# GpSimd makes the gated products of two FFN units in one instruction, with a ring of six units

## The chip, the core and the metric

The kernel runs on one core of one Trainium2 chip. The metric is the device time of one execution in microseconds (us). The profile's names of the engines are used beside the full ones: PE is TensorE (matmuls and transposes; PEld its weight loads), DVE is VectorE, ACT is ScalarE, POOL is GpSimd, SP is SyncE, which issues the DMAs here. Each engine takes its instructions in the order in which the kernel lists them for it; between engines only semaphores hold. So a late instruction delays everything behind it on its engine.

## The reference, cut to what matters

The input x has 8 images of 192 channels and 256 tokens. One layer norm and a delta-rule attention (12 heads of 16, chunks of 16 tokens) are followed by a second layer norm and a mixture-of-experts FFN:

```python
x = x + _L0_conv_ref(_ln_c(x), Wq, Wk, Wv, Wb, Wo)      # S_t = S_{t-1} + k_t u_t^T, o_t = S_t^T q_t, per head
t = _to_tokens(x)
t = t + _L0_ffn_ref(_ln_t(t), router_w, w_gate, w_up, w_down, ws_gate, ws_up, ws_down, sg_w, sg_b)
...
probs = jax.nn.softmax(x @ router_w, axis=-1)
gates, idx = jax.lax.top_k(probs, TOPK_ROUTED)           # 2 of E = 8 experts
g = jax.nn.silu(jnp.einsum('bsd,edh->bseh', x, w_gate))  # H = 192
u = jnp.einsum('bsd,edh->bseh', x, w_up)
expert_out = jnp.einsum('bseh,ehd->bsed', g * u, w_down)
routed = jnp.einsum('bse,bsed->bsd', dense_g, expert_out)
shared = jax.nn.silu(x @ ws_gate) * (x @ ws_up) @ ws_down  # HS = 768
alpha = jax.nn.sigmoid(x @ sg_w + sg_b)
return alpha * shared + (1.0 - alpha) * routed
```

All in float32. The kernel computes all eight experts for every token and gives the unselected ones a weight of zero. The `g * u` of the experts and of the shared part are the gated products that the change is about.

## The kernel before

The 256 tokens are cut into 16 chunks of 16 tokens; with 8 images a chunk has 128 rows, one for each partition. A software pipeline runs over steps c (about -3 to 18, a function `step(c, par)` for each engine): in step c the projections and norms of chunk c+3 and c+2 are made (functions `A_...`), the recurrence of chunk c runs, the attention output and second norm of chunk c-1 (`Fa_...`), and the FFN of chunks c-1 and c-2 (`Fb_...`, `unit`, `hidden`, `Fc_...`). `at(d, fn, ...)` calls fn for chunk c+d. In each `step` the order of the work of its engine is written out by hand.

**VectorE** runs the recurrence: 16 tokens of a chunk, four instructions each (L1425, L1427, L1429, L1433), which make 64 slots; the small jobs of the other stages stand between them at fixed slots (`others`). Slot 0 needs `fill` 0 of its chunk, a TensorE matmul (L403) that brings the keys into PSUM; slot 23 needs the attention output that GpSimd has summed (`Fa_otok`, L1238); slot 32 has the statistics of the second norm, slot 36 its bias (L1162), slot 43 the split of the normed tokens, slots 47 to 58 the router.

**The FFN** of a chunk has 12 units of 192 hidden columns (8 experts, 4 quarters of the shared part). For each unit TensorE makes gate and up (`Fb_up`, five matmuls, the last of them L440), ScalarE copies both to SBUF (`unit`: L713 silu, L714 scale) and GpSimd multiplies them (`hidden` on GpSimd, L1008). The copies go to a ring of `RING = 4` places in `sg` and `ug`: `unit` m waits until the product of unit m-4 has been made. The products go to `hid`, which holds half a chunk, six units. TensorE turns `hid` in five groups of up to four 128-column blocks (`Fb_turn` g, L448), all into one PSUM bank; ScalarE copies the bank (`hidden` g on ScalarE, L724); TensorE multiplies by the down weights (`Fb_down` g, L463). Turn g waits for the copy of turn g-1, and for as many units as its blocks cover: 3, 6, 8, 11 and 12 of them.

**GpSimd** also multiplies the states with the queries and sums them, in two halves for a chunk: `reading` (L963, two instructions) and `summing` (L970 three times, then L987). It makes `rs` for both norms (`rsqrt`, L952) and scales k, q and v (`A_kn`, `A_qn`, `A_vn` L920, `A_klo`). Its order in a steady step is: product 6, `rsqrt`, product 7, `reading` 0, products 8, 9, 10, `summing` 0, `A_kn`, product 11, `A_qn`, product 0 of the next chunk, `reading` 1, `summing` 1, `A_vn`, products 1 to 5, `A_klo`.

**ScalarE** has in the middle of a step two table loads (L748) around the exponentials and logarithms; in the order before, unit 11 stands behind them:

```python
at(-2, unit, 10)
at(-2, hidden, 1)
at(-3, Fc_out)
table(c + 2, LN_EXP)
at(2, A_inv)
table(c - 1, LN_EXP)
at(-1, Fa_exp)
table(0, SILU)
at(-2, hidden, 2)
at(-2, unit, 11)
at(-1, unit, 0)
```

**TensorE**'s order around it is: `Fb_turn` 1, `Fb_up` 11, `fill` 6, `Fb_up` 0 of the next chunk, `Fb_turn` 2, `Fb_down` 0, `fill` 7, `Fb_down` 1, `Fb_turn` 3, `Fb_down` 2, `fill` 0 of the next chunk, and so on.

Of the kernel before, what the change touches and what calls it, by code (L numbers as in the profile page):

```python
# [6 lines left out]
ALU = mybir.AluOpType  # L7
# [11 lines left out]
E, H, HS = 8, 192, 768  # L19
UN = E + HS // H  # L20
# [1 line left out]
KT = HID // P  # L22
GRP = [(0, 4), (4, 8), (8, 12), (12, 16), (16, 18)]
NG = len(GRP)
RING = 4
R = E + 2
NQK, NVB = 2 * C, C + NH
EARLY = 14
# [6 lines left out]
def build(nc, x, Wq, Wk, Wv, Wb, Wo, router_w, w_gate, w_up, w_down, ws_gate, ws_up, ws_down, sg_w, sg_b, out):  # L35
    ctx = ExitStack()
    with ctx:
# [51 lines left out]
        h = sb("h", [P, 2 * P])  # L89
# [474 lines left out]
        def _(act):  # L564
# [179 lines left out]
            def step(c, par):  # L744
                def table(n, name):

                    if (0 <= n < NC) and tables[0] != name:
                        nc.scalar.preload_act_table_set(name)  # L748
                        tables[0] = name

                at = partial(stage, c, par)
                if c == -3:
                    at(3, A_xs)
                    at(3, A_plus)
                    at(3, A_h)
                    at(3, A_xh)
                    at(3, A_hT)
                elif c == -2:
                    at(3, A_xs)
                    at(2, A_silu_v)  # L760
                    at(2, A_silu_qk)
                    at(2, A_sq)
                    table(0, LN_EXP)
                    at(2, A_inv)
                    at(2, A_khi)
                    at(3, A_plus)
                    at(3, A_h)
                    at(3, A_xh)
                    at(2, place, 0)
                    at(2, place, 1)  # L770
                    at(3, A_hT)
                    weights_hi0(5)
                    weights_hi0(6)
                elif c == -1:
                    at(3, A_xs)
                    weights_hi0(7)
                    weights_hi0(8)
                    table(0, SILU)
                    at(2, A_silu_v)
                    at(2, A_silu_qk)  # L780
                    weights_hi0(9)
                    at(2, A_sq)
                    table(0, LN_EXP)
                    at(2, A_inv)
                    at(3, A_plus)
                    weights_hi0(10)
                    at(3, A_h)
                    at(3, A_xh)
                    at(2, A_khi)
                    weights_hi0(11)  # L790
                    weights_hi1(0)
                    at(3, A_hT)
                    weights_hi1(1)
                    weights_hi1(2)
                elif c == 0:
                    weights_hi1(3)
                    at(3, A_xs)
                    table(0, SILU)
                    at(2, A_silu_v)
                    at(2, A_silu_qk)  # L800
                    at(2, A_sq)
                    weights_hi1(4)
                    weights_hi1(5)
                    at(1, place, 0)
                    table(0, LN_EXP)
                    at(2, A_inv)
                    at(3, A_plus)
                    weights_hi1(6)
                    weights_hi1(7)
                    at(3, A_h)  # L810
                    at(3, A_xh)
                    weights_hi1(8)
                    at(2, A_khi)
                    at(3, A_hT)
                elif c < NC:
                    if c == 1:
                        table(0, SILU)
                    if c > 1:
                        at(1, A_khi)
                    at(3, A_xs)  # L820
                    at(0, place, 1)
                    once(c, 1, weights_hi1, 9)
                    at(-2, unit, 3)
                    at(-2, unit, 4)
                    at(2, A_silu_qk)
                    at(2, A_sq)
                    at(2, A_silu_v)
                    once(c, 1, weights_hi1, 10)
                    at(-1, Fa_oc)
                    at(-2, unit, 5)  # L830
                    at(-2, unit, 6)
                    at(-2, hidden, 0)
                    at(-3, Fc_res)
                    at(-2, unit, 7)
                    once(c, 1, weights_hi1, 11)
                    at(-2, unit, 8)
                    at(-1, Fa_x1)
                    at(-1, Fa_h)
                    at(-2, unit, 9)
                    at(1, place, 0)  # L840
                    at(3, A_plus)
                    at(-1, Fa_hT)
                    at(-2, unit, 10)
                    at(-2, hidden, 1)
                    at(-3, Fc_out)
                    table(c + 2, LN_EXP)
                    at(2, A_inv)
                    table(c - 1, LN_EXP)
                    at(-1, Fa_exp)
                    table(0, SILU)  # L850
                    at(-2, hidden, 2)
                    at(-2, unit, 11)
                    at(-1, unit, 0)
                    at(3, A_h)
                    at(3, A_xh)
                    at(-2, hidden, 3)
                    at(-1, unit, 1)
                    at(-1, unit, 2)
                    at(3, A_hT)
                    at(-2, hidden, 4)  # L860
                else:
                    at(-2, unit, 3)
                    at(-2, unit, 4)
                    at(-3, Fc_res)
                    at(-1, Fa_oc)
                    at(-2, unit, 5)
                    at(-2, unit, 6)
                    at(-2, hidden, 0)
                    at(-2, unit, 7)
                    at(-2, unit, 8)  # L870
                    at(-1, Fa_x1)
                    at(-3, Fc_out)
                    at(-1, Fa_h)
                    at(-2, hidden, 1)
                    at(-2, unit, 9)
                    at(-1, Fa_hT)
# [7 lines that stand above are left out]
                    at(-1, unit, 1)  # L884
                    at(-2, hidden, 3)
                    at(-1, unit, 2)
                    at(-2, hidden, 4)
# [10 lines left out]
        def _(pool):  # L898
# [99 lines left out]
                tt(W1[:, columns(m)], raw1[:, columns(m)], spare(m), ALU.subtract).then_inc(s_w1, 1)  # L998

            def hidden(q, p, m):  # L1000
                pool.wait_ge(s_ug, q * UN + (m + 1))

                if m >= UN // 2 or later(q, 1):
                    last = ((m - UN // 2) % UN + 1) * H - 1
                    g = [lo * P <= last < hi * P for lo, hi in GRP].index(True)
                    pool.wait_ge(s_ht, q * NG + (g + 1 - (0 if m >= UN // 2 else NG)))
                r = m % (UN // 2)
                tt(hid[:, r * H:(r + 1) * H], sg[:, m % RING], ug[:, m % RING], ALU.mult).then_inc(s_hid, 1)  # L1008

            def step(c, par):  # L1010
                at = partial(stage, c, par)
# [39 lines left out]
                    weights_1(8)  # L1051
                elif c < NC:
                    once(c, 1, weights_1, 9)
                    at(-2, hidden, 6)
                    if c <= NC:
                        rsqrt(c)
                    at(-2, hidden, 7)
                    once(c, 1, weights_1, 10)
                    once(c, 1, weights_1, 11)
                    at(0, reading, 0)  # L1060
                    at(-2, hidden, 8)
                    at(-2, hidden, 9)
                    at(-2, hidden, 10)
                    at(0, summing, 0)
                    at(2, A_kn)
                    at(-2, hidden, 11)
                    at(2, A_qn)
                    at(-1, hidden, 0)
                    at(0, reading, 1)
                    at(0, summing, 1)  # L1070
                    at(2, A_vn)
                    at(-1, hidden, 1)
                    at(-1, hidden, 2)
                    at(-1, hidden, 3)
                    at(-1, hidden, 4)
                    at(-1, hidden, 5)
                    at(2, A_klo)
                else:
                    at(-2, hidden, 6)
                    if c <= NC:  # L1080
                        rsqrt(c)
                    at(-2, hidden, 7)
                    at(-2, hidden, 8)
                    at(-2, hidden, 9)
                    at(-2, hidden, 10)
                    at(-2, hidden, 11)
                    at(-1, hidden, 0)
                    at(-1, hidden, 1)
                    at(-1, hidden, 2)
                    at(-1, hidden, 3)  # L1090
                    at(-1, hidden, 4)
                    at(-1, hidden, 5)

            pool.memset(ident[:, :], 0.0).then_inc(s_id, 1)
            pool.wait_ge(s_id, 1)
# [378 lines left out]
```

## Time and profile before

| | |
|---|---|
| median of 3 runs | 482.03 us (480.83 to 482.6) |
| profiled execution | 479.88 us, of which the span from first to last instruction is 478.1 us |
| busy share of the span | DVE 88%, PE 87%, POOL 85%, PEld 80%, ACT 72% |
| granted TensorE clock | 0.96 in the mean; 1.00 from about 82 us on |

A busy share is a mean over the start (steps below 2, where there is no FFN work), the steady steps (from about 100 to 400 us, 25.15 to 25.45 us each) and the end after the recurrence (from 431 us on). A timeline row gives the start, the duration, the engine, the line, the operation, output and inputs by their tiles, the shape, how many instructions are merged in the row, and in brackets the idle time ahead of it with what ended that; the view names no idle time under 0.15 us.

### The profile page before, as it was taken

The numbers are of one execution on the slowest core, as the hardware profiler recorded it, in microseconds if no ns is written. First come the engines' busy times: TensorE is split into PE (matmuls) and PEld (weight loads), VectorE is DVE, ScalarE is ACT, GpSimd is POOL, SyncE is SP. The second block draws the span as 40 slices with busy tenths as digits, with TensorE's granted clock in tenths as the row PEclk, the third lists the DMA queues.
The fourth block names the chain that finished last, engine by engine and source line by source line (L and its number), as shares of the span: only waits on it lengthen the run. The fifth ranks groups of instructions, "written<-read, shape, count | busy, mean of one in ns | idle before, by whom it ended". The sixth has DMA issues, their size and how long they took to land.

```text
span 478.1 us, 10362 instructions
## 1 busy us (share of the span) xinstructions
PE 414.6 (87%) x2400; PEld 384.1 (80%) x2400; DVE 420.2 (88%) x2268; ACT 345.8 (72%) x998; POOL 407.4 (85%) x520
## 2 busy tenths in 40 slices
PE   1354456899999999999999999999999989899996
PEld 0333336798999999899999999999999979799895
DVE  4489989999999999999999999999999999996200
ACT  3699656585969787878778786969695848475762
POOL 4379888899999999999999999999999999986340
PEclk9998555999999999999999999999999999999999
DMA  6655673732233223232332323323322232200301
GB/s 162 169 129 124 147 187 84 179 91 83 80 84 91 81 78 92 72 92 63 93 81 76 98 71 90 85 83 93 83 73 92 77 95 86 89 1 1 116 2 16
DMA packets 43437, 42.91 MB, mean 90 GB/s; under 512 B 20144, under 2 KB 35184, under 8 KB 43376
## 3 DMA queue, kind: packets, MB, share of 16 engines
q1 hardware_dynamic: 42768, 42.05, 33.2%
q8 instruction: 19, 0.31, 0.3%
q14 instruction: 42, 0.34, 0.3%
q10 hardware_dynamic: 608, 0.21, 0.2%
HBM read 35.95 MB, written 6.29 MB: 88 GB/s over the span
## 4 chain that ended last, share of the span: by engine, by line
DVE 67%; PE 13%; issue 7%; SPq 4%; DMA 4%; ACT 2%; POOL 1%; DVEq 0%; ACTq 0%; POOLq 0%
DVE Pr L1425 15%; DVE bank L1429 15%; DVE u L1427 14%; DVE SH L1433 12%; PE bank L463 3%; DMA k_scratch<-khl 2%; PE bank L436 1%; PE bank L448 1%; DVE ss L1206 1%; SPq L242 1%; DMA q_scratch<-qn 1%; PE bank L440 1%; DVE vT L1213 1%; DVE otok L1238 1%; PE bank L438 1%
## 5 line engine op out<-in xcount | busy, mean ns | idle before, releaser
L1008 POOL TENSOR_TENSOR hid<-sg,ug 128x192 f32<-128x192 f32 x192 | 112.9, 608 | 21.2 <-ACT ug L714 18.0
L963 POOL TENSOR_TENSOR PQ<-SH,QB 128x768 f32<-128x768 f32 x62 | 112.7, 1840 | 0.9 <-DVE SH L1433 0.9
L713 ACT ACTIVATE sg<-bank 128x192 f32<-128x192 f32 x192 | 64.3, 335 | 60.7 <-PE bank L440 49.1
L970 POOL TENSOR_TENSOR PQ<-PQ 128x768 f32<-128x768 f32 (+2 forms) x93 | 103.0, 1107 | 6.0
L463 PE MATMUL bank<-Wd,hidT 128*128 128x192 f32 x576 | 106.6, 326 | 0.0
L1429 DVE TENSOR_TENSOR bank<-bank,u 128x96 f32<-128x96 f32 (+1 forms) x467 | 104.1, 263 | 0.6
L1427 DVE TENSOR_REDUCE u<-Pr 128x6 f32<-128x102 f32 (+1 forms) x437 | 102.1, 267 | 0.4
L1425 DVE TENSOR_TENSOR Pr<-SH,bank 128x96 f32<-128x96 f32 (+1 forms) x437 | 100.7, 264 | 1.7 <-issue 0.3
L1433 DVE TENSOR_TENSOR SH<-SH,bank 128x96 f32<-128x96 f32 (+1 forms) x467 | 101.5, 254 | 0.5 <-DVE st L1125 0.2
L463 PEld LDWEIGHTS bank<-Wd,hidT 128*128 128x128 f32 x576 | 94.5, 190 | 0.0
L436 PE MATMUL bank<-Whi,hiT 128*128 128x384 f32 (+1 forms) x192 | 72.5, 377 | 1.3 <-DVE loT L1168 1.3
L403 PE MATMUL bank<-KR,Sel 128*128 128x384 f32 x128 | 54.1, 424 | 20.0 <-DVE SH L1433 13.2
L440 PE MATMUL bank<-W,loT 128*128 128x384 f32 (+1 forms) x192 | 66.0, 344 | 0.0
L439 PE MATMUL bank<-W,hiT 128*128 128x384 f32 (+1 forms) x192 | 65.7, 342 | 0.0
L438 PE MATMUL bank<-Whi,loT 128*128 128x384 f32 (+1 forms) x192 | 65.7, 342 | 0.0
L437 PE MATMUL bank<-Wlo,hiT 128*128 128x384 f32 (+1 forms) x192 | 65.5, 341 | 0.0
L714 ACT ACTIVATE ug<-bank,gate 128x192 f32<-128x192 f32 x128 | 53.4, 417 | 0.0
L448 PE MATMUL bank<-ident,hid 128*128 128x128 f32 x288 | 45.6, 276 | 8.9 <-ACT hidT L724 8.2
L748 ACT ACT_TABLE_LOAD x38 | 48.8, 1283 | 0.7
L724 ACT ACTIVATE hidT<-bank 128x512 f32<-128x512 f32 (+1 forms) x80 | 45.7, 572 | 2.2 <-PE bank L448 2.0
L448 PEld LDWEIGHTS bank<-ident,hid 128*128 128x128 f32 x288 | 33.9, 141 | 15.0 <-issue 11.8
L403 PEld LDWEIGHTS bank<-KR,Sel 128*128 128x128 f32 x128 | 25.9, 203 | 24.7 <-DVE SH L1433 16.4
(143 smaller groups left out, 814.5 us busy)
## 6 DMA issues: line engine op xcount, KB each, us to landing
QB<-q_scratch SPq DMA_DIRECT2D x64, 384.0 KB
k_scratch<-khl SPq DMA_DIRECT2D x64, 48.0 KB, 1.7
KR<-k_scratch SPq DMA_DIRECT2D x32, 96.0 KB, 2.4
q_scratch<-qn SPq DMA_DIRECT2D x64, 24.0 KB, 1.8
Wd<-in_L_ffn_w_down_dram SPq DMA_DIRECT2D x4, 288.0 KB, 9.4
out_dram<-xT SPq DMA_DIRECT2D x1, 896.0 KB, 4.1
Wlo_unsplit<-in_L_ffn_w_gate_dram SPq DMA_DIRECT2D x2, 384.0 KB, 4.6
Wlo_unsplit<-in_L_ffn_w_up_dram SPq DMA_DIRECT2D x2, 384.0 KB, 5.5
```

The costliest lines, as they stand in the source:

```text
L403: mm(bKB[f % 2][:, 0:2 * BR * G], Sel[:, f].rearrange("p b x e -> p (b x e)"), KR[:, p, :], start=True, stop=True).then_inc(s_fill, 1)
L436: mm(to, hiT[:, p, 0:P], Whi0[:, w], start=True, stop=False)
L440: mm(to, loT[:, p, P:2 * P], W1[:, w], start=False, stop=True).then_inc(s_up, 1)
L448: last = tr(bHt[:, (k - lo) * P:(k - lo + 1) * P], hid[:, k % (KT // 2) * P:(k % (KT // 2) + 1) * P], ident[:, :])
L463: last = mm(bDn[:, 0:C], hidT[:, turn_half(g), k - lo, :], Wd[:, k, :], start=False, stop=(k == KT - 1))
L963: tt(PQ[:, at * BR * HP:(at + n) * BR * HP].rearrange("p (i b h) d -> p i b (h d)", i=n, b=BR), SH[:, lo:lo + n].rearrange("p i b h d -> p ...
L970: chained(tt(PQ[:, :, 0:w], PQ[:, :, 0:w], PQ[:, :, w:2 * w], ALU.add))
L1008: tt(hid[:, r * H:(r + 1) * H], sg[:, m % RING], ug[:, m % RING], ALU.mult).then_inc(s_hid, 1)
L1425: v = each(slot, lambda lo, hi: count(tt(Pr[:, lo:hi, i, :, 0:D], prev[:, lo:hi], KB[:, lo:hi], ALU.mult)), Sb)
L1427: v = each(slot + 1, lambda lo, hi: count(nc.vector.tensor_reduce(u[:, i % 2, lo:hi], Pr[:, lo:hi, i], X, ALU.add, negate=True)), v)
L1429: v = each(slot + 2, lambda lo, hi: count(tt(KB[:, lo:hi], KB[:, lo:hi], u[:, i % 2, lo:hi].unsqueeze(3).to_broadcast([P, hi - lo, HP, D]) ...
L1433: ins = tt(SH[:, i, lo:hi], prev[:, lo:hi], KB[:, lo:hi], ALU.add)
```

## The change

`RING` becomes 6, so that two neighbouring units lie side by side and never wrap. GpSimd's `hidden` takes two units: it waits for both copies and for the turn that frees the place of the second, and makes 384 columns in one instruction. The six pairs of a chunk stand at these places of GpSimd's step: `rsqrt` first, then pair 6/7, `reading` 0, pairs 8/9 and 10/11, `summing` 0, `A_kn`, `A_qn`, `reading` 1, `summing` 1, `A_vn`, pairs 0/1, 2/3, 4/5, `A_klo`. On ScalarE unit 11 moves from behind `hidden` 2 to ahead of `Fc_out`, in the steps below 16. The waits of `Fb_turn` are left as they are; since the count of products goes up by two, turn 0 now waits for 4 units and turn 3 for 12.

```diff
-RING = 4
+RING = 6
...
                     at(-2, unit, 10)
                     at(-2, hidden, 1)
+                    at(-2, unit, 11)
                     at(-3, Fc_out)
                     table(c + 2, LN_EXP)
                     at(2, A_inv)
...
                     table(0, SILU)
                     at(-2, hidden, 2)
-                    at(-2, unit, 11)
                     at(-1, unit, 0)
...
             def hidden(q, p, m):
-                pool.wait_ge(s_ug, q * UN + (m + 1))
+                pool.wait_ge(s_ug, q * UN + (m + 2))
                 if m >= UN // 2 or later(q, 1):
-                    last = ((m - UN // 2) % UN + 1) * H - 1
+                    last = ((m + 1 - UN // 2) % UN + 1) * H - 1
                     g = [lo * P <= last < hi * P for lo, hi in GRP].index(True)
                     pool.wait_ge(s_ht, q * NG + (g + 1 - (0 if m >= UN // 2 else NG)))
-                r = m % (UN // 2)
-                tt(hid[:, r * H:(r + 1) * H], sg[:, m % RING], ug[:, m % RING], ALU.mult).then_inc(s_hid, 1)
+                r, s = m % (UN // 2), m % RING
+                tt(hid[:, r * H:(r + 2) * H].rearrange("p (m h) -> p m h", m=2), sg[:, s:s + 2], ug[:, s:s + 2],
+                   ALU.mult).then_inc(s_hid, 2)
...
-                    at(-2, hidden, 6)
                     if c <= NC:
                         rsqrt(c)
-                    at(-2, hidden, 7)
+                    at(-2, hidden, 6)
...
                     at(0, reading, 0)
                     at(-2, hidden, 8)
-                    at(-2, hidden, 9)
                     at(-2, hidden, 10)
                     at(0, summing, 0)
                     at(2, A_kn)
-                    at(-2, hidden, 11)
                     at(2, A_qn)
-                    at(-1, hidden, 0)
                     at(0, reading, 1)
                     at(0, summing, 1)
                     at(2, A_vn)
-                    at(-1, hidden, 1)
+                    at(-1, hidden, 0)
                     at(-1, hidden, 2)
-                    at(-1, hidden, 3)
                     at(-1, hidden, 4)
-                    at(-1, hidden, 5)
                     at(2, A_klo)
```

In the steps from 16 on GpSimd has the same pairs in the same order, without the other work.

## Rows read from the trace of the kernel before

**Rows 1.** The page: busy time of the engines, and the chain that ended last.

```profile
PE 414.6 (87%) x2400; PEld 384.1 (80%) x2400; DVE 420.2 (88%) x2268; ACT 345.8 (72%) x998; POOL 407.4 (85%) x520
...
DVE 67%; PE 13%; issue 7%; SPq 4%; DMA 4%; ACT 2%; POOL 1%; DVEq 0%; ACTq 0%; POOLq 0%
```

**Rows 2.** Busy us of PE, PEld, DVE, ACT, POOL in one step.

```profile
239.57:264.72 25.15, 24.46 (x152) 23.33 (x151) 25.01 (x140) 19.96 (x60) 24.03 (x31) 1.00 0.30 84
```

**Rows 3.** Timeline of VectorE: slot 0, and one reduction in two places.

```profile
256.27 0.42 DVE L1425 TENSOR_TENSOR Pr<-SH,bank 128x96 f32<-128x96 f32 x2
...
256.61 0.42 DVE L1427 TENSOR_REDUCE u<-Pr 128x6 f32<-128x102 f32 x2
...
269.28 0.42 DVE L1427 TENSOR_REDUCE u<-Pr 128x6 f32<-128x102 f32 x2
```

**Rows 4.** Timeline of TensorE: turns 3, 0, 2 and 3, fill 0, unit 11.

```profile
253.93 0.63 PE L448 MATMUL bank<-ident,hid 128*128 128x128 f32 x4 [0.69 <-ACT hidT L724]
...
255.57 0.47 PE L403 MATMUL bank<-KR,Sel 128*128 128x384 f32 x1
...
266.34 0.66 PE L448 MATMUL bank<-ident,hid 128*128 128x128 f32 x4
...
273.51 0.34 PE L440 MATMUL bank<-W,loT 128*128 128x384 f32 x1
...
274.79 0.60 PE L448 MATMUL bank<-ident,hid 128*128 128x128 f32 x4
...
279.15 0.63 PE L448 MATMUL bank<-ident,hid 128*128 128x128 f32 x4 [0.66 <-ACT hidT L724]
```

**Rows 5.** Timeline of ScalarE: unit 10 to unit 0 of the next chunk.

```profile
272.83 0.38 ACT L713 ACTIVATE sg<-bank 128x192 f32<-128x192 f32 x1
...
273.35 0.67 ACT L724 ACTIVATE hidT<-bank 128x512 f32<-128x512 f32 x1
...
273.83 0.35 ACT L735 ACTIVATE xT<-bank 128x128 f32<-128x128 f32 x1
...
278.41 0.60 ACT L724 ACTIVATE hidT<-bank 128x512 f32<-128x512 f32 x1
...
280.17 0.33 ACT L713 ACTIVATE sg<-bank 128x192 f32<-128x192 f32 x1 [0.62 <-DVE gate L1301]
```

**Rows 6.** Waits over the whole run: us in total, times, longest.

```profile
PE bank L448 <- ACT hidT L724: 8.2, 12, 1.0
```

**Rows 7.** Instruction groups of GpSimd: busy us, mean ns of one.

```profile
L1008 POOL TENSOR_TENSOR hid<-sg,ug 128x192 f32<-128x192 f32 x192 | 112.9, 608 | 21.2 <-ACT ug L714 18.0 <-PE bank L448 2.0
...
L993 POOL TENSOR_TENSOR Wlo<-Wlo_unsplit,Whi 128x384 fp32r<-128x384 f32 x7 | 7.3, 1060 | 1.6 <-ACT Whi L692 1.6
...
L998 POOL TENSOR_TENSOR W<-W_unsplit,hidT 128x384 fp32r<-128x384 f32 x2 | 1.7, 862 | 0.0
```

**Rows 8.** Timeline of GpSimd: vn, products, rsqrt, summing 0 and reading 1.

```profile
264.60 0.51 POOL L920 TENSOR_TENSOR vn<-v,inv 128x192 f32<-128x192 f32 x1
...
265.07 2.80 POOL L1008 TENSOR_TENSOR hid<-sg,ug 128x192 f32<-128x192 f32 x5
...
269.62 0.70 POOL L952 TENSOR_TENSOR rs<-ve,neg_half 128x2 f32<-128x2 f32 x1 [0.64 <-DVE ve L1156]
...
276.24 3.46 POOL L970 TENSOR_TENSOR PQ<-PQ 128x768 f32<-128x768 f32 x3
...
282.45 3.62 POOL L963 TENSOR_TENSOR PQ<-SH,QB 128x768 f32<-128x768 f32 x2
```

**Rows 9.** Timeline of GpSimd and TensorE in the last steps.

```profile
414.92 2.25 POOL L1008 TENSOR_TENSOR hid<-sg,ug 128x192 f32<-128x192 f32 x4
...
432.14 3.05 POOL L1008 TENSOR_TENSOR hid<-sg,ug 128x192 f32<-128x192 f32 x2 [0.70 <-ACT ug L714]
...
468.12 0.59 POOL L1008 TENSOR_TENSOR hid<-sg,ug 128x192 f32<-128x192 f32 x1 [1.93 <-ACT ug L714]
...
468.94 0.60 PE L448 MATMUL bank<-ident,hid 128*128 128x128 f32 x4
```

More of the change, by code:

```diff
@@ L1071, in step @@
                     at(2, A_vn)
-                    at(-1, hidden, 1)
+                    at(-1, hidden, 0)
                     at(-1, hidden, 2)
-                    at(-1, hidden, 3)
                     at(-1, hidden, 4)
-                    at(-1, hidden, 5)
                     at(2, A_klo)
                 else:
-                    at(-2, hidden, 6)
                     if c <= NC:
                         rsqrt(c)
-                    at(-2, hidden, 7)
+                    at(-2, hidden, 6)
                     at(-2, hidden, 8)
-                    at(-2, hidden, 9)
                     at(-2, hidden, 10)
-                    at(-2, hidden, 11)
                     at(-1, hidden, 0)
-                    at(-1, hidden, 1)
                     at(-1, hidden, 2)
-                    at(-1, hidden, 3)
                     at(-1, hidden, 4)
-                    at(-1, hidden, 5)
             pool.memset(ident[:, :], 0.0).then_inc(s_id, 1)
```

## The prediction, made before the change was run

> **What bounds the kernel now.** I read the page first. VectorE is the busiest engine and has 67% of the chain that ended last, TensorE 13%, GpSimd 1% [rows 1]. The shares hide how close the others are, so the next view is the busy time in one steady step: in 25.15 us VectorE works 25.01, TensorE 24.46, GpSimd 24.03, ScalarE 19.96 [rows 2]. VectorE sets the step; it has no time to give back, and TensorE and GpSimd have 0.7 and 1.1 us. So a change that frees GpSimd gains nothing in these steps unless VectorE waited for it, and the question is what it makes late. For that I read the timelines around everything that the change moves.
>
> The waits say where TensorE has its spare time: twelve times it waits at a turn for ScalarE's copy of the turn before, 8.2 us in all, the longest 1.0 [rows 6]. That longest one is after the recurrence; the other eleven, one in each steady step, have 7.2/11 = 0.66 us. In the timeline they stand at turn 3: it starts at 253.93 and 279.15, and both times TensorE sat idle for 0.69 and 0.66 us until ScalarE's `hidden` 2 was done [rows 4]. Between these two rows no idle time stands in TensorE's timeline. Behind turn 3 come `Fb_down` 2 and then `fill` 0, which ends at 255.57 + 0.47 = 256.04; VectorE starts slot 0 of that chunk at 256.27 [rows 3, 4]. So VectorE has a cushion of 0.23 us to TensorE there, and none of the idle time ahead of turn 3 can be called spare: it is ended by ScalarE.
>
> **The change part by part.**
>
> *Unit 11 on ScalarE.* Before, ScalarE runs without a gap from unit 10 (272.83) through `hidden` 1 (273.35), `Fc_out` (273.83), two table loads and the exponentials to `hidden` 2 (278.41); then unit 11, and then it idles 0.62 us until the gates let unit 0 start at 280.17 [rows 5]. There unit 11 was free: that idle time covered it. Now it stands ahead of `Fc_out`. A unit takes 273.35 - 272.83 = 0.52 us from start to start [rows 5]. It also has to wait for its matmuls, the last of which ends at 273.51 + 0.34 = 273.85 [rows 4], so about 273.89 instead of 273.83. Everything from `Fc_out` on is late by 0.06 + 0.52 = 0.58 us: `hidden` 2 starts at 278.99, turn 3 at 279.73. From the end of unit 11's matmuls to turn 3 it was 279.15 - 273.85 = 5.30 us; it becomes 5.88.
>
> This closes a loop. Turn 3 at 253.93 to the end of unit 11's matmuls at 273.85 is 19.92 us of TensorE in which the view names no idle time [rows 4]; unit 11, the table loads, `hidden` 2 and turn 3 are 5.88 more. A step takes 25.80 us by this loop, against 25.21 from turn 3 to turn 3 before (19.92 + 5.30). So 0.59 us more in each of the eleven steps that the waits count: 6.5 us. The cushion of 0.23 us at slot 0 comes off once: 6.3 us.
>
> *Pairs on GpSimd.* A single product has a mean of 608 ns, and five in a row take 2.80 us, 0.56 each from start to start [rows 7, 8]. For 384 columns the trace has other instructions of two inputs: 1060 ns and 862 ns in the mean [rows 7]. I take 1.0 us, nearer the dearer one, or 0.955 from start to start with the singles' overlap of 0.05; the bounds are 0.81 (from 862) and 1.12 (two singles, no gain). A pair so saves 0.16 us, six of them 1.0 us of GpSimd's 24.03. Nothing is subtracted from the time for that, since GpSimd isn't on the path [rows 1, 2].
>
> *Pair 10/11 ahead of `summing` 0.* It waits for turn 2, which ends at 274.79 + 0.60 = 275.39 [rows 4]; behind it queue `summing` 0, `A_kn`, `A_qn` and `reading` 1. The pair runs to about 276.4. Before, `summing` 0 started at 276.24 and `reading` 1 at 282.45, with products 11 and 0 (1.12 us) between them [rows 8]. Without these it is 276.4 + 6.21 - 1.12 = 281.5, 0.95 us earlier than before, about when VectorE has the states for it. I take nothing for it; the cover is the two products that left this stretch, and without it the wait would cost its 0.2 us at `reading` 1.
>
> *Products 0 to 3 behind `A_vn`, and turn 0.* Turn 0 needs pair 2/3 now, not product 2, and product 0 no longer stands ahead of `reading` 1. Before, turn 0 came 266.34 - 265.07 = 1.27 us after the first product behind `vn` [rows 4, 8]; two pairs take 1.91 and the hand-over some 0.1, so 0.75 us more. `reading` 1 is up to 0.95 us earlier, and TensorE comes 0.59 us later in each step, so the pairs just make it. The loop through GpSimd: from `rsqrt` (269.62, one step back 244.47) to the first product behind `vn` (265.07) it is 20.6 us with six single products [rows 8]; three pairs in their place make it 20.1; two pairs and the hand-over lead to turn 0 (22.1), and from turn 0 to the next `rsqrt` it is 269.62 - 266.34 = 3.28 us [rows 4, 8]. Sum 25.4 us, under 25.80: no further cost at 0.955 us a pair. At 1.12 it is 25.4 + 5 x 0.165 = 26.2, and GpSimd sets the step.
>
> *`rsqrt` ahead of product 6.* It waits 0.64 us for VectorE before [rows 8]; that wait stays, and product 6 is done with 7 behind it, in time for turn 2. Nothing. The ring of six only lets ScalarE run further ahead; it has no wait for `hidden` products to lose in these steps. Nothing. No DMA is moved; the k and q that GpSimd makes go out in the next step.
>
> *The last steps.* In step 15 there is no `vn`, and the products start at 414.92, as soon as the sums are done [rows 9]; `reading` 1 cannot be earlier there, so turn 0 is late by the 0.75 us less what the row gives in slack, I take 0.6. ScalarE's unit 11 adds up to its 0.52 once more there; I take 0.4. From there to the end the chain is TensorE's, and nothing gives it back: 1.0 us. At the very end product 11 starts at 468.12 and turn 3 at 468.94 [rows 9]; pair 10/11 ends at 468.12 + 1.0 + 0.05, so turn 3 is 0.2 us late, and the end with it.
>
> VectorE's own sums of the last half chunk run beside GpSimd's products at 432.14, where two of them take 3.05 us instead of 1.12 [rows 9]: they hold each other up. A pair holds on for 0.4 us longer than a single; I take nothing, since TensorE is by then 1.0 us later than VectorE, and 0.4 as the bound. The Trainium skill, SBUF — State Buffer, section "Who interferes with whom", says of this that a VectorE instruction with two SBUF inputs and a GpSimd instruction that reads SBUF shut each other out for a whole instruction, whoever is first. This row agrees; by the rule alone the sum would have the 0.4 us on top.
>
> Sum: 6.3 + 1.0 + 0.2 = 7.5 us. On the profiled execution's 479.88 us that is 487.4; that execution is 2.15 us under the median of the runs shown, and on the median of 482.03 it is **489.5 us**.
>
> **The rivals.**
>
> *Pairs dear: GpSimd sets the step.* If a pair costs its two singles (1.12), the step is 26.2 us, 0.4 more than forecast, in eleven steps 4.4 us: 493.9. For it: products and sums leave GpSimd only 1.1 us [rows 2]. Against: both instructions of 384 columns were cheaper than two singles [rows 7]. It decides from 1.04 us a pair on (25.80 - 25.4 = 0.4, over five pairs 0.08 above 0.955).
>
> *No change: TensorE absorbs it.* If the 19.92 us hold 0.6 us of waits that are each too short for the view to name, TensorE makes up for the late turn 3 and VectorE goes on at 25.15: only the last steps' 1.2 us stay, 483.2. Half of it absorbed gives 11 x 0.29 - 0.2 + 1.2 = 4.2 us, 486.2. For it: the view is silent under 0.15 us. Against: TensorE's 24.46 us busy of 25.15 leave 0.69, and that is the wait at turn 3 itself [rows 2, 4].
>
> *Faster: VectorE gains from a less busy GpSimd.* If VectorE's instructions were held up by GpSimd's reads, 1.0 us less of these in a step could give VectorE up to as much: in thirteen steps 13 us, 469. It decides if VectorE's instructions are shorter where GpSimd idles. At 269.28, in GpSimd's wait from 268.98 to 269.62, two reductions take 0.42 us, at 256.61 beside its work 0.42 as well [rows 3, 8]. So I see nothing of it. The skill's section named above states that an instruction with at most one SBUF input doesn't contend, which is what these are.
>
> **How the numbers follow.** Half a per cent, 2.4 us, is about what a measurement of this kernel can tell from no change. The forecast, with half absorbed and with some of the dear pair's cost, has 0.72; the dear pair in full 0.12; no change 0.11; faster 0.05. Slower has so 0.84, the same 0.11, faster 0.05. The time is the forecast's, 489.5. The range goes down to 484.0, below half absorbed and short of no change, and up to 493.5, just under the dear pair in full.
>
> **What would show it.** Right: steady steps of some 25.8 us; TensorE's idle time ahead of turn 3 near 1.25 us, ended by ScalarE's `hidden` 2; VectorE idle at slot 0 until `fill` 0, some 0.5 us a step; ScalarE's unit 11 at once behind its matmuls; pairs of about 1.0 us; turn 0 not waiting for GpSimd before step 14. Wrong: steps of 25.15 with VectorE without gaps (absorbed); turn 0 waiting for GpSimd's pair 2/3 or VectorE for `Fa_otok` in each step (GpSimd sets it); VectorE's instructions shorter than before.

## The result, and the profile after

The changed kernel takes 489.78 us in the median of 4 runs (489.66 to 491.03), the kernel before beside it 481.6 us (480.83 to 482.6, 4 runs). The ratio is 1.0192, with an interval of 1.0169 to 1.0216: slower by 8.2 us. The prediction was 489.5 us. The profiled execution took 489.77 us, its span is 488.0.

The page of the changed kernel: busy time of the engines, the chain that ended last, and the group of the products (busy us, mean ns of one, idle time before them):

```profile
PE 418.1 (86%) x2400; PEld 386.9 (79%) x2400; DVE 424.0 (87%) x2268; ACT 346.8 (71%) x998; POOL 392.6 (80%) x424
...
PE 12%; DVE 7%; ACT 2%; issue 1%; POOL 1%; POOLq 0%; ACTq 0%; DVEq 0%
...
L1008 POOL TENSOR_TENSOR hid<-sg,ug 128x384 f32<-128x384 f32 x96 | 95.9, 1011 | 39.8 <-ACT ug L714 18.2
```

The chain names 23% of the span only, the end; it says nothing of the steady steps this time. A pair costs 1011 ns, two single products cost 1216 [rows 7]. GpSimd did become freer, by 0.2 us a pair, and the kernel slower, so the time has to be looked for where the other engines wait. One steady step of the changed kernel, from slot 0 to slot 0 (busy us of PE, PEld, DVE, ACT, POOL; then the clock):

```profile
259.00:284.76 25.76, 24.55 (x152) 23.41 (x151) 25.18 (x140) 19.95 (x61) 23.22 (x25) 1.00 0.29 82
```

The step is 25.76 us, was 25.15 [rows 2]. GpSimd has 0.8 us less to do in it, VectorE 0.17 and TensorE 0.09 more: no engine has become the bound by its work (VectorE, the busiest, idles 0.58 us of the step). The idle times say who waits. TensorE's timeline of the same step, turns 3, 0 and 3, `fill` 0 and the last matmul of unit 11:

```profile
256.86 0.63 PE L448 MATMUL bank<-ident,hid 128*128 128x128 f32 x4 [1.21 <-ACT hidT L724]
...
258.49 0.47 PE L403 MATMUL bank<-KR,Sel 128*128 128x384 f32 x1
...
269.28 0.66 PE L448 MATMUL bank<-ident,hid 128*128 128x128 f32 x4
...
276.45 0.34 PE L440 MATMUL bank<-W,loT 128*128 128x384 f32 x1
...
282.62 0.63 PE L448 MATMUL bank<-ident,hid 128*128 128x128 f32 x4 [1.22 <-ACT hidT L724]
```

The idle time ahead of turn 3 is 1.21 and 1.22 us, was 0.69 and 0.66 [rows 4]; turn 0 has none. ScalarE's timeline there, `hidden` 1, unit 11, `Fc_out`, `hidden` 2 and unit 0 of the next chunk:

```profile
276.28 0.66 ACT L724 ACTIVATE hidT<-bank 128x512 f32<-128x512 f32 x1
276.83 0.33 ACT L713 ACTIVATE sg<-bank 128x192 f32<-128x192 f32 x1
...
277.36 0.28 ACT L735 ACTIVATE xT<-bank 128x128 f32<-128x128 f32 x1
...
281.88 0.60 ACT L724 ACTIVATE hidT<-bank 128x512 f32<-128x512 f32 x1
...
282.92 0.33 ACT L713 ACTIVATE sg<-bank 128x192 f32<-128x192 f32 x1 [0.45 <-DVE gate L1290]
```

Unit 11 now starts 0.04 us behind its matmuls (276.45 + 0.34 = 276.79), `Fc_out` behind it, and from the end of those matmuls to turn 3 it is 282.62 - 276.79 = 5.83 us, was 5.30. The idle time ahead of unit 0 is 0.45 us, still ended by the gates: unit 11, gone from there, brings unit 0 nothing. The waits of the whole run (us in total, times, longest):

```profile
PE bank L448 <- ACT hidT L724: 15.7, 15, 1.2
```

Was 8.2 us in 12 [rows 6]. VectorE at slot 0 of chunks 3, 9, 14 and 15 (lines shift by 11 to the numbers of before):

```profile
104.33 0.42 DVE L1414 TENSOR_TENSOR Pr<-SH,bank 128x96 f32<-128x96 f32 x2
...
259.00 0.42 DVE L1414 TENSOR_TENSOR Pr<-SH,bank 128x96 f32<-128x96 f32 x2 [0.24 <-PE bank L403]
...
387.61 0.42 DVE L1414 TENSOR_TENSOR Pr<-SH,bank 128x96 f32<-128x96 f32 x2 [0.24 <-PE bank L403]
...
416.01 0.42 DVE L1414 TENSOR_TENSOR Pr<-SH,bank 128x96 f32<-128x96 f32 x2
```

and in the trace of before at slot 0 of chunks 3, 14 and 15:

```profile
104.86 0.42 DVE L1425 TENSOR_TENSOR Pr<-SH,bank 128x96 f32<-128x96 f32 x2
...
382.32 0.42 DVE L1425 TENSOR_TENSOR Pr<-SH,bank 128x96 f32<-128x96 f32 x2
...
407.23 0.42 DVE L1425 TENSOR_TENSOR Pr<-SH,bank 128x96 f32<-128x96 f32 x2
```

From chunk 3 to chunk 14 it is 283.28 us, 25.75 a step; before it was 277.46 us, 25.22 a step. So the eleven steps cost 5.8 us. From chunk 14 to 15 it is 28.40 us, where before it is 24.91: **one step, step 14, costs 3.5 us**, and this was not foreseen. TensorE's timeline of it:

```profile
396.63 0.33 PE L350 MATMUL bank<-ident,otok 128*128 128x128 f32 x1 [0.98 <-DVE otok L1227]
...
398.01 1.12 PE L448 MATMUL bank<-ident,hid 128*128 128x128 f32 x4 [0.77 <-POOL hid L1008]
...
402.72 0.52 PE L440 MATMUL bank<-W,loT 128*128 128x384 f32 x1
...
405.62 0.34 PE L440 MATMUL bank<-W,loT 128*128 128x384 f32 x1
```

and stretches of 2 us (as above; the clock is the third figure from the end):

```profile
396.00:398.00 2.00, 0.61 (x3) 0.36 (x3) 2.00 (x13) 0.89 (x5) 1.96 (x3) 1.00 0.51 138
398.00:400.00 2.00, 1.99 (x8) 1.89 (x8) 1.58 (x8) 1.40 (x5) 1.55 (x2) 0.50 0.17 47
400.00:402.00 2.00, 2.00 (x6) 1.23 (x5) 0.55 (x3) 0.00 (x0) 0.00 (x0) 0.50 0.31 74
402.00:404.00 2.00, 2.00 (x8) 2.00 (x8) 2.00 (x12) 0.64 (x2) 0.70 (x1) 0.50 0.10 24
404.00:406.00 2.00, 2.00 (x11) 2.00 (x11) 1.74 (x11) 1.12 (x5) 1.95 (x2) 0.79 0.46 124
```

The four matmuls of turn 0, 0.66 us in the step shown above, take 1.12, a matmul of 384 columns 0.52 in place of 0.34: the granted clock was 0.50, which is 1.2 of the 2.4 GHz, from 398.0 to 404.8. Ahead of it TensorE had idled 0.98 us for the attention output and 0.77 for GpSimd's pair 2/3, and was busy 0.61 of 2 us. VectorE then waits for TensorE, the first time for the statistics of the second norm:

```profile
401.38 0.37 DVE L1135 BATCH_NORM_STATS2 st<-bank 128x6 f32<-128x192 f32 x1 [1.56 <-PE bank L418]
```

The end, pair 10/11 of the last chunk and turn 3 behind it:

```profile
477.74 0.99 POOL L1008 TENSOR_TENSOR hid<-sg,ug 128x384 f32<-128x384 f32 x1 [2.19 <-ACT ug L714]
478.79 0.66 PE L448 MATMUL bank<-ident,hid 128*128 128x128 f32 x4
```

The ledger of the profiled executions: 0.5 us earlier at chunk 3, +5.8 in eleven steps, +3.5 in step 14, +1.1 from there to the end: 9.9 us between the spans. The medians differ by 8.2, since the profiled execution of before is 1.7 us under its median.

### The profile page after: what moved, and what is told of

The parts are those of the page before. It is cut to its first block and busy times, and to the rows that moved or that the text cites. A ratio compares the mean times of both kernels' runs of the same rounds, so it can differ in the third digit from the quotient of the medians.

```text
span 488.0 us, 10188 instructions
## 1 busy us (share of the span) xinstructions
PE 418.1 (86%) x2400; PEld 386.9 (79%) x2400; DVE 424.0 (87%) x2268; ACT 346.8 (71%) x998; POOL 392.6 (80%) x424
## 5 line engine op out<-in xcount | busy, mean ns | idle before, releaser
L1008 POOL TENSOR_TENSOR hid<-sg,ug 128x384 f32<-128x384 f32 x96 | 95.9, 1011 | 39.8 <-ACT ug L714 18.2
L713 ACT ACTIVATE sg<-bank 128x192 f32<-128x192 f32 x192 | 64.5, 336 | 70.9 <-PE bank L440 60.0
```

The lines of the kernel that those rows point to most:

```text
L1008: tt(hid[:, r * H:(r + 2) * H].rearrange("p (m h) -> p m h", m=2), sg[:, s:s + 2], ug[:, s:s + 2], ALU.mult).then_inc(s_hid, 2)
```

## The experiments

Two parts of the change can lengthen the step: unit 11 on ScalarE (TensorE's loop through `hidden` 2) and the pairs on GpSimd (turn 0 waits for four units). The step given below is the mean from slot 0 of chunk 3 to that of chunk 14 in each profile (25.22 us before, 25.75 with the change); each ratio is to the median of the kernel before on the same chip.

**Unit 11 alone** (in the kernel before):

```diff
 at(-2, hidden, 1)
+at(-2, unit, 11)
...
 at(-2, hidden, 2)
-at(-2, unit, 11)
```

> The kernel before with one edit: ScalarE's unit 11 ahead of Fc_out (ring of four, single products, GpSimd's order as before). If the loop over ScalarE's table loads and turn 3 is the cause: steps of 25.75 to 25.8 us, TensorE idle 1.2 us ahead of each turn 3, 5 to 6.5 us more at slot 0 of chunk 14, no half-clock stretch in step 14 (turn 0 waits 0.36 us there as before); 487 to 489 us. If GpSimd's pairs and their waits are the cause: steps of 25.2 us and 481 to 483 us.

Measured: 485.66 us beside 480.68, ratio 1.0109 [1.0074, 1.0145]; the step is 25.70 us. Turn 3 of this kernel:

```profile
282.65 0.63 PE L448 MATMUL bank<-ident,hid 128*128 128x128 f32 x4 [1.22 <-ACT hidT L724]
```

The same 1.22 us of idle time as with the whole change, and 11 x (25.70 - 25.22) = 5.3 us accounts for the 5.0 by which the medians differ; the time is below the 487 to 489 us that I expected. The move of unit 11, by itself, makes the steady steps what they are. Step 14 holds no stretch at half clock here.

**The pairs alone**, with ScalarE's old order and pair 10/11 where product 11 was (against the changed kernel):

```diff
-at(-2, unit, 11)            # ScalarE: back behind hidden 2
-at(-2, hidden, 10)          # GpSimd: from ahead of summing 0 ...
 at(0, summing, 0)
 at(2, A_kn)
+at(-2, hidden, 10)          # ... to behind A_kn
```

> The changed kernel with ScalarE's order of before and pair 10/11 where product 11 stood, behind A_kn. If the ScalarE loop is the cause of the longer steps: steps of 25.15 to 25.2 us, TensorE idle 0.66 us ahead of turn 3; what stays is step 14 (turn 0 waits some 0.8 us for pair 2/3, and if that is what brings TensorE's clock to 1.2 GHz there, 3.4 us) and 0.3 us at the end; 482 to 486 us. If the pairs cause it: steps of 25.7 us, 488 to 490 us.

Measured: 529.87 us, ratio 1.1016 [1.0956, 1.1076], a step of 28.95 us. I expected 482 to 490 us: missed by far. I had overlooked that turn 3, which waited for 11 units before, now waits for pair 10/11. TensorE, ScalarE and GpSimd there (turn 3; `hidden` 2 and unit 11; `summing` 0 and pair 10/11):

```profile
307.75 1.11 PE L448 MATMUL bank<-ident,hid 128*128 128x128 f32 x4 [3.02 <-POOL hid L1008]
```

```profile
304.67 0.60 ACT L724 ACTIVATE hidT<-bank 128x512 f32<-128x512 f32 x1
305.16 0.32 ACT L713 ACTIVATE sg<-bank 128x192 f32<-128x192 f32 x1
305.37 0.42 ACT L714 ACTIVATE ug<-bank,rden 128x192 f32<-128x192 f32 x1
```

```profile
302.09 3.46 POOL L970 TENSOR_TENSOR PQ<-PQ 128x768 f32<-128x768 f32 x3
...
306.69 1.00 POOL L1008 TENSOR_TENSOR hid<-sg,ug 128x384 f32<-128x384 f32 x1
```

ScalarE's unit 11 ends at 305.79, but GpSimd comes to the pair only at 306.69, behind `summing` 0 and `A_kn`; turn 3 waits 3.02 us, and then runs at half clock, 1.11 us. From 105 to 430 us the granted clock has a mean of 0.94, where it is 1.00 in the kernel before, so part of the 48 us is the clock. This kernel doesn't price the pairs. The last 0.90 us of turn 3's wait come from the pair's place on GpSimd, not from ScalarE's order, and no run has pair 10/11 ahead of `summing` 0 with ScalarE's old order. An estimate for that from these rows: the pair could start at 305.79, and turn 3 at 305.79 + 1.00 + 0.06 = 306.85, which is 2.2 us behind the start of `hidden` 2, where it was 279.15 - 278.41 = 0.74 [rows 4, 5]. **By this estimate pair 10/11 without unit 11 ahead of `Fc_out` costs 1.4 us a step, more than the 0.5 us of the move**; it is argued, not shown.

**The cost of unit 11 taken back**: `hidden` 2 ahead of the last table load, so that it needn't wait for it (against the changed kernel, in the steps below 16):

```diff
-table(0, SILU)
 at(-2, hidden, 2)
+table(0, SILU)
```

> The changed kernel with ScalarE's hidden 2 ahead of the table load that it stood behind (steps below 16). By the ScalarE loop that takes 1.28 us out of the chain from unit 11 to turn 3, more than the 0.59 that the move put in: steps of 25.15 to 25.2 us, TensorE's idle time ahead of turn 3 gone or under 0.3 us, 5 to 6 us back; with step 14's stretch 484 us, without it 481. By the pairs as cause nothing comes back: 489 to 490 us.

Measured: 487.23 us, ratio 1.0139 [1.01, 1.0177]; a step of 25.59, where I expected 25.15 to 25.2: missed. The wait at turn 3 went, but the step hardly got shorter. Turn 0 and turn 3 of one step:

```profile
270.28 0.66 PE L448 MATMUL bank<-ident,hid 128*128 128x128 f32 x4 [0.53 <-POOL hid L1008]
...
282.22 0.60 PE L448 MATMUL bank<-ident,hid 128*128 128x128 f32 x4
```

and GpSimd's `rsqrt` one step earlier, pairs 0/1 and 2/3, and `rsqrt`:

```profile
247.62 0.70 POOL L952 TENSOR_TENSOR rs<-ve,neg_half 128x2 f32<-128x2 f32 x1 [1.19 <-DVE ve L1145]
...
268.26 1.96 POOL L1008 TENSOR_TENSOR hid<-sg,ug 128x384 f32<-128x384 f32 x2
...
273.29 0.70 POOL L952 TENSOR_TENSOR rs<-ve,neg_half 128x2 f32<-128x2 f32 x1 [1.36 <-DVE ve L1145]
```

Now turn 0 waits for pair 2/3 in each step (14 such waits, 7.9 us). The loop of the prediction can be read off: from `rsqrt` to the first pair it is 20.64 us, in which GpSimd has no idle time that the view names, to turn 0 2.02, to the next `rsqrt` 3.01, in sum 25.67 here and 25.59 in the mean of the steps. **Behind TensorE's loop of 25.76 stands GpSimd's of 25.59**; removing the first gives 0.17 us, not 0.5.

**Step 14**: in step 13 alone, `A_vn` behind pair 2/3, so that turn 0 of step 14 finds its units earlier.

```diff
-at(2, A_vn)
+if c != 13:
+    at(2, A_vn)
 at(-1, hidden, 0)
 at(-1, hidden, 2)
+once(c, 13, stage, c, par, 2, A_vn)
```

> The changed kernel with A_vn behind pair 2/3 in step 13 alone. Turn 0 of step 14 then waits 0.77 - 0.47 = 0.3 us for GpSimd, not 0.77. If that wait is what lets TensorE's clock fall to 1.2 GHz from 398 to 405 us: no such stretch, 3.4 us less, 486.4 us. If the fall has another cause: 489 to 490 us, the stretch stays.

Measured: 486.91 us, ratio 1.0142 [1.0106, 1.0179], steps of 25.75. Turn 0 of step 14:

```profile
397.45 0.66 PE L448 MATMUL bank<-ident,hid 128*128 128x128 f32 x4 [0.30 <-POOL hid L1008]
```

The wait is 0.30 us, TensorE keeps its full clock (1.00 in every stretch from 398 to 404), and from slot 0 of chunk 14 (387.52) to that of chunk 15 (412.44) it is 24.92 us, as before the change (24.91). Without the longer wait step 14 costs nothing in this profile.

**The changed kernel again**, beside the next three:

> The changed kernel once more, beside the others on one chip. If the half-clock stretch of step 14 belongs to it: 1.015 to 1.02 of the kernel before, the stretch in this profile again, some 3 us over the run with A_vn behind pair 2/3. If it was a chance of the first profile: no stretch, 1.011 to 1.014.

Measured: 488.97 us (486.32 to 491.1) beside 481.35, ratio 1.0153 [1.0104, 1.0201]. The half clock is there again, for 6.83 us, behind 0.98 and 0.74 us of idle time, and this step 14 takes 28.34 us:

```profile
399.32 0.67 PE L448 MATMUL bank<-ident,hid 128*128 128x128 f32 x4 [0.74 <-POOL hid L1008]
```

The medians can't confirm its price: this ratio's interval holds the 1.0142 of the kernel without the half clock, and whether each of the four executions has the half clock is not known, since only one was profiled.

**Each pair as two single products**, at the same places, with ring and order of the change:

```diff
-r, s = m % (UN // 2), m % RING
-tt(hid[:, r * H:(r + 2) * H].rearrange("p (m h) -> p m h", m=2), sg[:, s:s + 2], ug[:, s:s + 2],
-   ALU.mult).then_inc(s_hid, 2)
+for n in (m, m + 1):
+    r, s = n % (UN // 2), n % RING
+    tt(hid[:, r * H:(r + 1) * H], sg[:, s], ug[:, s], ALU.mult).then_inc(s_hid, 1)
```

> The changed kernel with each pair made by two single products, one behind the other, all else as it is. By the loop through GpSimd (25.4 us a step with pairs of 0.955 us; 25.45 to 25.5 measured where ScalarE's chain was shortened) five pairs dearer by 0.165 us make 26.2 to 26.3 us a step, above the ScalarE loop's 25.76: some 5 us more at slot 0 of chunk 14, 494 us, with TensorE waiting at turn 0 for GpSimd. If GpSimd is clear of the path: 490 us, steps of 25.76.

Measured: 486.43 us, ratio 1.0106 [1.0065, 1.0146], steps of 25.75, where I expected 26.2: missed. Single products count one by one, so turn 0 needs three of them again, not two pairs. From the trace of this kernel GpSimd's loop is an estimated 20.95 us from `rsqrt` to the first product, 3 x 0.56 + 0.1 to turn 0 and 2.90 to `rsqrt`, in sum 25.6, just under TensorE's 25.76. In the steady steps making two units in one instruction saves nothing that counts. Turn 0 of step 14 waits 0.52 us here, and the clock stays at 1.00.

**Both loops undone**: `hidden` 2 ahead of the table load in all steps, and units 0 to 5 as two triples (the last argument is the count of units), so that turn 0 (3 units) waits for one instruction:

```diff
-at(-1, hidden, 0)
-at(-1, hidden, 2)
-at(-1, hidden, 4)
+at(-1, hidden, 0, 3)
+at(-1, hidden, 3, 3)
```

> The changed kernel with hidden 2 of ScalarE ahead of the table load (the last steps too) and units 0 to 5 as two products of three units in place of three pairs. Both loops are then under VectorE's 25.15 us: ScalarE's at 24.5, GpSimd's at 20.1 + 1.4 + 0.1 + 3.3 = 24.9. If these two loops are all that the change cost: steps of 25.15 to 25.2 us, VectorE without gaps, 479.5 to 482 us. If something else of the pairs or of the larger ring costs time: steps above 25.3, 483 us or more.

Measured: 479.95 us beside 481.35, ratio 0.9984 [0.9961, 1.0006], 10 runs; steps of 25.22. One step, and its turn 3:

```profile
257.50:282.70 25.20, 24.81 (x150) 22.96 (x150) 24.87 (x139) 19.45 (x61) 22.84 (x24) 1.00 0.27 78
```

```profile
278.98 0.60 PE L448 MATMUL bank<-ident,hid 128*128 128x128 f32 x4
```

VectorE works 24.87 of 25.20 us, the idle time at turn 3 is gone: with both waits away, the step is VectorE's again, as before. The ring of six and pairs 6/7 to 10/11 are still in this kernel, so in this order they cost the steps nothing.

**`hidden` 2 ahead of the table load in the kernel before**, all steps:

> The kernel before with hidden 2 of ScalarE ahead of the table load, in all steps. TensorE's 0.66 us ahead of turn 3 go, but VectorE sets the step, so steps stay at 25.15 us; in step 16, after the recurrence, the wait of 0.96 us at turn 3 is on the path and goes: 0.5 to 1 us less, 479.7 to 480.2 us. If TensorE set the steps before: 0.3 us less in each, 477 us.

Measured: 480.61 us, ratio 0.9978 [0.9955, 1.0000], 10 runs; steps of 25.22. The 0.66 us ahead of turn 3 are gone from the trace, and not one step is shorter for it: with VectorE as the bound this wait had been free. It was the place where a delay of ScalarE counts at once, not a loss. Only in step 16, behind the recurrence, was such a wait on the path: its 0.96 us are gone, and from slot 0 of chunk 15 to the end it is 69.8 us, was 70.9.

**Pairs for units 0 to 9 only**, with ScalarE's old order; products 10 and 11 single (last argument 1), 10 ahead of `summing` 0 and 11 behind `A_kn`:

```diff
-at(-2, unit, 11)               # ScalarE: back behind hidden 2
-at(-2, hidden, 10)
+at(-2, hidden, 10, 1)
 at(0, summing, 0)
 at(2, A_kn)
+at(-2, hidden, 11, 1)
```

> Ring of six and pairs for units 0 to 9, products 10 and 11 single in their places of before, ScalarE's unit 11 in its place of before. If the 48 us of the run with six pairs and ScalarE's old order came from turn 3, which then waited for unit 11 through pair 10/11: that wait is gone (turn 3 waits for product 10 only), TensorE idles 0.66 us or less ahead of turn 3. The loop through GpSimd is then 20.6 - 0.33 + 1.91 + 0.1 + 3.28 = 25.56 us a step: 0.4 us more than before in each, TensorE waiting at turn 0 for pair 2/3; 484 to 488 us. If pairs cost nothing in the steps: 25.15 us, 481 to 482. If the pairs themselves cost the 48 us: over 500.

Measured: 489.52 us beside 480.63, ratio 1.0169 [1.0132, 1.0206], steps of 25.69, a little above the 25.56 and the 484 to 488 us expected. Turns 0 and 3:

```profile
269.17 0.66 PE L448 MATMUL bank<-ident,hid 128*128 128x128 f32 x4 [0.48 <-POOL hid L1008]
...
281.98 0.63 PE L448 MATMUL bank<-ident,hid 128*128 128x128 f32 x4 [0.69 <-ACT hidT L724]
```

Turn 3 waits as before the change, 0.69 us; turn 0 waits 0.48 for a pair. Without the move of unit 11 the pairs alone make the step 25.69 us. The half clock in step 14 is there, behind a wait of 1.09 us at turn 0.

**The triples once more**, with more executions:

> The version with products of three units and hidden 2 ahead of the table load, in more rounds. By the loops: VectorE sets the step as in the kernel before, the last steps lose the 0.96 us wait of step 16: 0.998 of the kernel before. If it is no better than the kernel before: an interval around 1.

Measured: 479.6 us beside 480.63, ratio 0.9978 [0.9959, 0.9996], 12 runs. Some 1 us faster than before, if at all; the move of `hidden` 2 alone gave as much, by the wait in step 16.

The six kernels that tell the loops apart:

| ScalarE ahead of turn 3 | units that turn 0 waits for | step |
|---|---|---|
| old order | 3 (before) | 25.22 us |
| unit 11 ahead | 3 (unit 11 alone) | 25.70 |
| old order | 4, in two pairs (pairs for 0 to 9) | 25.69 |
| unit 11 ahead | 4, in two pairs (the change) | 25.75 |
| unit 11 ahead, `hidden` 2 ahead of the load | 4, in two pairs | 25.59 |
| unit 11 ahead, `hidden` 2 ahead of the load | 3, in one triple (triples) | 25.22 |

## Why the prediction was right, step by step

**Unit 11 on ScalarE: right.** The loop was put at 25.80 us a step, with 5.88 from unit 11's matmuls to turn 3 and an idle time near 1.25; it is 25.76, 5.83 and 1.22. The experiment with this edit alone has the same step within 0.06 us and turn 3's wait to the hundredth. The eleven steps cost 5.8 us, not 6.3. (The loop before is 19.92 + 5.30 = 25.22 us, not 25.21.) No slack of TensorE's absorbed it: that rival is out, in every profile where unit 11 stands ahead of the table loads and `hidden` 2 behind them.

**VectorE at slot 0: too large.** Its idle time there is 0.24 us a step, not 0.5. Of the 0.61 us by which the step grew, 0.17 are longer busy time of VectorE and 0.2 are idle time elsewhere, in pieces that I did not trace one by one.

**The price of a pair: right**, 1011 ns where 1.0 us was taken; the rival of the dear pair, 1.12 us, is out.

**GpSimd's loop: too short by 0.2 us, and hidden.** It was worked out at 25.4 us and closes at 25.59 once nothing covers it. The term that was too small is from `rsqrt` to the first pair, 20.64 us in the step shown where 20.1 was taken. More than half of that is a misreading. The prediction put the `rsqrt` of one step back at 269.62 - 25.15 = 244.47, but the steps before take 25.15 to 25.45 us, and the trace of before has it earlier:

```profile
244.17 0.70 POOL L952 TENSOR_TENSOR rs<-ve,neg_half 128x2 f32<-128x2 f32 x1 [0.42 <-DVE ve L1156]
```

So with six single products the stretch was 265.07 - 244.17 = 20.90 us, not 20.6. The rest is that three pairs took 0.26 us out of it, not 0.5. The term from turn 0 to `rsqrt`, 3.28 us in that long step, is 3.01 here and makes up for part of it. Under TensorE's loop it costs nothing, as was said, but the margin was 0.17 us, not 0.4.

**Pair 10/11 ahead of `summing` 0: no cost on GpSimd, as taken.** Left out was what ties it to ScalarE: turn 3 waits for 12 units now, so unit 11 behind `hidden` 2 would hold it back, by 1.4 us a step if the estimate above holds. The prediction treated these as two edits.

**Step 14: missed.** The sum holds nothing for it. Turn 0 waited there for GpSimd before the change already, 0.36 us:

```profile
392.31 0.66 PE L448 MATMUL bank<-ident,hid 128*128 128x128 f32 x4 [0.36 <-POOL hid L1008]
```

The pairs made it 0.77; what it costs is 3.5 us, because TensorE's clock fell. In the profile with the wait shortened to 0.30 us all of it is gone. The ratio there is 1.0142, against 1.0192 and 1.0153 in the two measurements of the change; the intervals overlap, so the price is read from the profiles alone.

**The last steps and the end: right**, 1.1 us for 1.2. Counted from slot 0 of chunk 15, turn 0 of step 15 is 0.59 us later (0.6 taken), turn 3 a further 0.16 (0.4 taken for ScalarE's unit 11); at the very end turn 3 comes 0.23 us later behind the start of the last product (0.2 taken).

**Faster because GpSimd reads less: out.** VectorE's instructions of the recurrence are 0.42 us before and after.

The sum was 7.5 us, the medians differ by 8.2. The agreement is partly luck. Between the profiles the sum would have had to be 9.9: 3.5 for step 14, less 0.5 in the steps, 0.5 at the start and 0.1 at the end. Against the medians 1.7 of this fall away, by which the profiled execution of before lies under its median. The mechanism that carries most of the time, 5.8 of 9.9 us in the profiles, is the one that was predicted.

**What stays open.** Why the clock fell: three profiles with turn 0 of step 14 waiting 0.74 to 1.09 us have the half clock behind it, those with 0.52 us or less don't; but the one with `hidden` 2 ahead of the table load waited 1.00 us and kept its full clock, as shown below. So a long wait at turn 0 goes with it and does not decide it; with one profile of each kernel, and two of the change, chance isn't excluded. Slot 0 of chunk 3 lies up to 3 us apart among the kernels (104.25 to 107.36, and 109.57 with the pairs alone); I did not trace why. And no run has pair 10/11 ahead of `summing` 0 with ScalarE's old order.

## What to carry to other kernels

An idle time that one engine ends in each step, though the engine beside it is the bound, is not a reserve: work it out as a loop (from the wait round to itself) and see how far it is from the step; here 0.66 us of idle time left nothing, and 0.53 us of delay (5.83 - 5.30) cost 0.53 in each step. Two such loops do not add up, the longer sets the step, and taking one away shows the next: price all of them before undoing one. When an instruction makes two units and counts both at its end, look at every wait that counted single units; turn 0 went from three to four, turn 3 from eleven to twelve, and the second, by the estimate above, makes the costly move worth its price.

## What the runs showed of the hardware

In step 14 two idle times of TensorE, each under 1 us, went ahead of 6.8 us at half clock. Two such, 0.97 and 1.00 us, in the kernel with `hidden` 2 ahead of the table load left it at full clock, though a third of 0.95 us stood 3 us ahead of them (turn 0 in TensorE's timeline, and stretches of 2 us):

```profile
398.59 0.66 PE L448 MATMUL bank<-ident,hid 128*128 128x128 f32 x4 [1.00 <-POOL hid L1008]
```

```profile
398.00:400.00 2.00, 1.41 (x9) 1.19 (x10) 1.76 (x10) 1.64 (x6) 2.00 (x3) 1.00 0.32 88
400.00:402.00 2.00, 2.00 (x11) 1.77 (x12) 1.64 (x10) 0.57 (x3) 0.77 (x2) 1.00 0.24 59
```

The Trainium skill, TensorE: Matmul & The Clock Gate, section "A second HAM failure mode: psum-queue depth-cycling", tells of another kernel in which short, frequent idle times between groups of matmuls make the clock swing between its two levels. The changed kernel's trace agrees in part: behind 0.98 and 0.77 us the clock fell, but once; the last rows show that such idle times need not do it.

GpSimd's product costs a fixed part and a part by columns, as far as three widths show it: 0.60 us for 192 columns, 1.00 for 384, and for 576, in the kernel with triples:

```profile
267.34 1.40 POOL L1008 TENSOR_TENSOR hid<-sg,ug 128x576 f32<-128x576 f32 x1 [0.65 <-issue]
```

That is 0.40 us for each 192 columns and 0.20 for each instruction, so by this estimate six pairs save no more than 6 x 0.2 = 1.2 us of GpSimd's step; its busy time fell by 0.8.
